# A 16-expert layer computed routed instead of dense: rows listed by expert in pieces of 64, two pieces per pass

## The reference

```python
scores = jax.nn.softmax(h @ gate_w.T, axis=-1)
topk_w, topk_idx = jax.lax.top_k(scores, 6)
cw = zeros((T, 16)).at[arange(T)[:, None], topk_idx].add(topk_w)
for e in range(16):
    g = h @ w_gate[e].T                       # 256 -> 176
    u = h @ w_up[e].T                         # 256 -> 176
    y = y + cw[:, e:e + 1] * (silu(g) * u @ w_down[e].T)
```

## Time and profile before

| | |
|---|---|
| median of 3 runs | 858.1 us (857.93 to 858.56) |
| profiled execution | 859.15 us, its span 857.4 us |
| granted clock of TensorE, mean | 0.988 |
| busy: TensorE, its weight loads | 814.1, 570.0 us |
| busy: VectorE, ScalarE, GpSimd | 457.1, 318.5, 161.8 us |
| DMA | 72.07 MB, mean 84 GB/s |

### The profile page before, as it was taken

One profiled execution on the slowest core, in us unless ns is written; L12 is line 12 of the kernel. 1 busy time (PEld: TensorE's weight loads), 2 busy tenths in 40 slices (PEclk: granted clock), 3 DMA queues, 4 the chain that ended last, 5 costly groups with the idle time before them and its releaser, 6 DMA issues.

```text
span 857.4 us, 12754 instructions
## 1 busy us (share of the span) xinstructions
PE 814.1 (95%) x4543; PEld 570.0 (66%) x4543; DVE 457.1 (53%) x1054; ACT 318.5 (37%) x651; POOL 161.8 (19%) x256
## 2 busy tenths in 40 slices
PE   6988799889969999999999999999999999999998
PEld 3566566676657786677777777777766655555557
DVE  5999866766522226866464566467443252322223
ACT  3987777545113324442423334333402211111111
POOL 3643744112510034111111111111100000000000
PEclk9998999999989999999999999999999999999999
DMA  4002780091253322022101011101123344344431
GB/s 141 2 2 34 240 269 2 22 255 33 84 169 105 93 68 68 19 62 87 31 26 37 25 38 29 33 25 37 52 94 120 119 123 124 126 154 130 134 100 49
DMA packets 63958, 72.07 MB, mean 84 GB/s; under 512 B 14201, under 2 KB 48505, under 8 KB 63897
## 3 DMA queue, kind: packets, MB, share of 16 engines
q1 hardware_dynamic: 59048, 64.06, 24.8%
q0 software_dynamic: 1536, 4.20, 1.5%
q10 hardware_dynamic: 3312, 3.02, 1.1%
HBM read 55.45 MB, written 14.75 MB: 82 GB/s over the span
## 4 chain that ended last, share of the span: by engine, by line
PE 77%; DVE 10%; issue 4%; ACT 4%; POOL 2%; DMA 2%; SPq 0%; DVEq 0%; ACTq 0%; POOLq 0%
PE bank L936 10%; PE bank L898 10%; PE bank L912 10%; PE bank L1113 8%; PE bank L1080 7%; PE bank L975 6%; PE bank L961 6%; PE bank L636 3%; PE bank L1863 3%; PE bank L658 2%; PE bank L1847 2%; PE bank L1820 2%; PE bank L1648 2%; PE bank L985 1%; DVE sh L2401 1%
## 5 line engine op out<-in xcount | busy, mean ns | idle before, releaser
L1145 ACT ACTIVATE arena<-bank 128x512 f32<-128x512 f32 (+1 forms) x64 | 34.7, 544 | 217.6 <-PE bank L898 205.5
L1253 DVE TENSOR_TENSOR arena<-arena,bank 128x512 f32<-128x512 f32 (+1 forms) x47 | 30.7, 654 | 151.7 <-PE bank L912 151.7
L936 PE MATMUL bank<-arena 128*128 128x256 f32 x448 | 108.9, 384 | 1.4 <-DVE arena L1251 1.3
L936 PEld LDWEIGHTS bank<-arena 128*128 128x128 f32 x448 | 85.8, 193 | 32.1 <-issue 20.1
L898 PE MATMUL bank<-xnT,arena 128*128 128x512 f32 (+1 forms) x256 | 107.0, 540 | 0.0
L912 PE MATMUL bank<-xnT,arena 128*128 128x512 f32 (+1 forms) x256 | 106.6, 539 | 0.0
L1214 ACT ACTIVATE arena<-bank 128x512 f32<-128x512 f32 (+1 forms) x96 | 46.8, 524 | 135.2 <-PE bank L1080 135.2
L861 POOL TENSOR_TENSOR arena<-arena,causal_t 128x256 f32<-128x256 f32 x64 | 45.1, 725 | 238.7 <-ACT arena L1219 238.7
L912 PEld LDWEIGHTS bank<-xnT,arena 128*128 128x128 f32 x256 | 48.6, 190 | 47.6 <-issue 45.9
L1113 PEld LDWEIGHTS bank<-arena 128*128 128x128 f32 x640 | 76.3, 191 | 4.4 <-POOL arena L861 2.9
L1113 PE MATMUL bank<-arena 128*128 128x129 f32 x640 | 77.0, 275 | 1.9 <-POOL arena L861 1.9
(11 more groups left out here) (236 smaller groups left out, 1178.8 us busy)
## 6 DMA issues: line engine op xcount, KB each, us to landing
arena<-in_w_gu SPq DMA_DIRECT2D x60, 256.0 KB, 3.6
rows_in<-place SPq DMA_DIRECT2D x5, 1664.0 KB, 14.6
arena<-in_w_dn SPq DMA_DIRECT2D x56, 128.0 KB, 3.5
arena<-in_wq SPq DMA_DIRECT2D x32, 128.0 KB, 2.2
arena<-in_wo SPq DMA_DIRECT2D x32, 128.0 KB, 2.0
arena<-cw_rows SPq DMA_DIRECT2D x15, 256.0 KB, 3.5
arena<-rows_in SPq DMA_DIRECT2D x23, 128.0 KB, 2.1
rows_out<-arena ACTq DMA_DIRECT2D x23, 128.0 KB, 1.7
```

The costliest lines, as they stand in the source:

```text
L936: mm = nc.tensor.matmul(Y[s][half][l // 2][:, (l % 2) * DIM:(l % 2 + 1) * DIM], hh[:, M % 3, j * P:(j + 1) * P], w_dn[:, slot_of(M), :], s ...
L1145: nc.scalar.activation(sg[:, M % 2, 0:n], ring(M)[0][:, 0:n], ACT.Silu).then_inc(s_silu, 1)
```

## The change

The layer is routed. For each half the 512 x 6 = 3,072 (token, expert) pairs are listed by expert, every expert's list rounded up to pieces of 64 rows: at most 64 pieces, so NP1 = 32 passes of two pieces, 64 passes J for both halves. In a pass, piece u (0 or 1) has the array's columns 64u to 64u + 63 and its own expert's weights.

- Routing: `route_b3` now ends in a mask; `places1` counts ranks and totals (TensorE), `rows1_read`, `rows1_index`, `rows1_weights`, `rows1_edges`, `rows1_table`, `rows1_owner` (VectorE) make the row index of each pair, its weight, and a table of weight offsets per piece. Half 0 has this in attention heads 20 to 28, its norm and logits three to four heads earlier than before; half 1 in passes 2 to 16.
- Rows: GpSimd scatters the normed rows (1,088 bytes, with a code for token and rank) into `rows1` by 24 indirect DMAs per half: four behind the masks of each of heads 25 to 30 for half 0, all 24 in pass R0 = 10 for half 1, groups of four waiting for the one before. SyncE fills `rows1` with zeros before (16 DMAs, heads 2 to 17), reads a pass's 128 rows (`load_rows`, five ahead), and reads back the codes (`ext`).
- Weights: all 16 experts' weights are loaded once, in heads 2 to 23, and stay. ScalarE and VectorE copy piece 1's (704 columns, 88 x 512) to a fixed place each pass (`pair_copy_gu`, `pair_copy_dn`), at an offset read into a register; TensorE reads two offsets per pass for piece 0.
- Results: a pass's 128 rows are copied out of PSUM (`pair_y`) and scattered by GpSimd to `ret` in token order (`send_back`); SyncE reads the six results of a half's tokens back (`load_back`, half 0 in pass 50, half 1 after the last), and VectorE adds them with their weights, 24 adds per half (`add_back`), half 0's in passes 52 to 63.
- Gone: the tile loop of the layer, the spreading of weights by DMA, `cw_turn`, `cw_evac`.

The diff, cut to its core:

```diff
+        def pair_gate_up(self, pe, J, off):
+            pe.wait_ge(s_pxe, NB + J + 1)
+            if J < 2:
+                pe.wait_ge(s_th, 3 * NH - 2 + J)
+            else:
+                pe.wait_ge(s_pm, NB + J - 1)
...
+            pe.wait_ge(s_wbg, J + 1)
+            wide = lambda w: w.rearrange("p (y k n) -> p k y n", y=2, k=KD)
+            w = wide(w1_gu[:, bass.ds(off[0], GU1)]), wide(wbg[:, J % 2, :])
+            for k in range(KD):
+                for u in range(2):
+                    mm = nc.tensor.matmul(p_gu[J % 2][u * HR:(u + 1) * HR, 0:2 * FE].rearrange("p (y n) -> p y n", y=2),
+                                          pxT[:, J % 2, k, u * HR:(u + 1) * HR], w[u][:, k, :, :],
+                                          start=(k == 0), stop=(k == KD - 1), skip_group_check=True)
+            mm.then_inc(s_pgu, 1)
...
+        def pair_down(self, pe, J, off):
+            pe.wait_ge(s_pte, NB + J + 1)
...
+            pe.wait_ge(s_wbd, J + 1)
...
+            for q in range(2):
+                for u in range(2):
+                    mm = nc.tensor.matmul(p_y[u * HR:(u + 1) * HR, :], phT[0:HB, J % 2, q, u * HR:(u + 1) * HR],
+                                          w[u][:, q, :], start=(q == 0), stop=(q == 1), skip_group_check=True)
...
+        def pair_y(self, act, J):
+            act.wait_ge(s_pyd, NB + J + 1)
+            if J >= NY:
+                act.wait_ge(s_ret, RE0 + 64 * ((J - NY) // 4 + 1))
+            nc.scalar.copy(py[J % NY], p_y).then_inc(s_pye, 1)
...
+        def send_rows(self, pool, h, groups):
+            for g in groups:
+                if g == 0:
+                    pool.wait_ge(s_pl, DI1[h])
...
+                else:
+                    pool.wait_ge(s_rows, SC + SC1 * h + 64 * g)
+                for i in range(4 * g, 4 * g + 4):
+                    nc.gpsimd.indirect_dma_start(rows1[h], bass.IndirectOffsetOnAxis(ap=sidx1[:, h, i % K1, i // K1:i // K1 + 1], axis=0),
+                                                 xa[h][:, i // K1, :], None).then_inc(s_rows, 16)
+
+        def send_back(self, pool, J):
+            h, j = J // NP1, J % NP1
+            if j == 0:
+                pool.wait_ge(s_rx1, h + 1)
+            if J and J % 4 == 0:
+                pool.wait_ge(s_ret, RE0 + 16 * J)
+            pool.wait_ge(s_pye, NB + J + 1)
...
                 if n < NH - 1:
                     self.queries(pe, n + 1)
                 else:
-                    self.gate_up(pe, F1, attn0)
+                    self.pair_turn(pe, 0)
                 if n:
                     self.project(pe, n - 1)
...
+                if n == NH - 1:
+                    self.pair_turn(pe, 1)
+                    offs = [owners(J) for J in range(3)]
+                    self.pair_gate_up(pe, 0, offs[0])
...
+            for J in range(2 * NP1):
+                if J + 2 < 2 * NP1:
+                    self.pair_turn(pe, J + 2)
+                if J + 1 < 2 * NP1:
+                    self.pair_gate_up(pe, J + 1, offs[J + 1])
+                if J + 3 < 2 * NP1:
+                    offs.append(owners(J + 3))
+                self.pair_hidden(pe, J)
+                if J:
+                    self.pair_down(pe, J - 1, offs[J - 1])
...
+            self.pair_silu(act, 0)
+            for J in range(2 * NP1):
+                if J + 2 < 2 * NP1:
+                    self.pair_copy_gu(act, J + 2)
+                    self.pair_x(act, J + 2)
+                if J + 1 < 2 * NP1:
+                    self.pair_silu(act, J + 1)
+                if J:
+                    self.pair_y(act, J - 1)
+                if J == 3:
                     self.ln_std(act, 10)
                     self.ln_std(act, 11)
...
+            for J in range(2 * NP1):
+                if J == R0:
+                    self.send_rows(pool, 1, range(K1))
+                self.send_back(pool, J)
```

More of the change, by code:

```diff
@@ L338, in cuts_of @@
         return [(a, b, min((i * P + a) // F, MOE_GATES[s] - 1)) for a, b in zip(cuts, cuts[1:])]
-    pieces = {M: cuts_of(1, IT[M][2]) for M in range(F1, F1END)}
     NBL = [16 * ((NB - j + 2) // 3) for j in range(3)]
-    cb_n = {M: NBL[M % 3] + 16 * sum(len(pieces[m]) for m in range(M, F1 - 1, -3)) for M in range(F1, F1END)}
     LEAD = 3
@@ new lines, in pick, with rows1_read @@
+        def pick(self, dve, c, src):
+            for k in range(K1):
+                ins = nc.vector.scalar_tensor_tensor(out=c.tk[:, k, :, :], in0=c.lg[:], scalar=float(k), in1=src,
+                                                     op0=ALU.is_equal, op1=ALU.mult)
+                s_r.by(ins)
+            dve.wait_ge(s_r.sem, s_r.n)
+        def rows1_read(self, dve, h):
+            dve.wait_ge(s_pf, 2 + h + 1)
+            nc.vector.tensor_copy(scr[2 + h].pos_cnt, p_pos[h][:, 0:5 * E1]).then_inc(s_pl, 1)
@@ new lines, in owner, with pair_copy_gu @@
+        def owner(self, eng, J, u, y):
+            h, q = J // NP1, 2 * (J % NP1) + u
+            if q == u:
+                eng.wait_ge(s_tab, 3 + 2 * (h + 1))
+            return eng.value_load(tab1[0:1, h, y, q:q + 1], min_val=0, max_val=(E1 - 1) * (GU1, 2 * DIM)[y])
+        def pair_copy_gu(self, act, J):
+            off = self.owner(act, J, 1, 0)
+            if J >= 2:
+                act.wait_ge(s_pgu, NB + J - 1)
+            elif J == 0:
+                act.wait_ge(s_qr, len(order))
+                act.wait_ge(s_we, n_we1)
+            nc.scalar.copy(wbg[:, J % 2, :], w1_gu[:, bass.ds(off, GU1)]).then_inc(s_wbg, 1)
@@ L749, in sp, with load_back @@
+        def load_back(self, sp, h):
+            sp.wait_ge(s_ret, RE0 + 16 * (h + 1) * NP1)
+            for k in range(K1):
+                sp.dma_start(ys[k], ret[h][1 + k * HALF:1 + (k + 1) * HALF, :].rearrange("(t p) d -> p t d", p=P)).then_inc(s_ys[k], 16)
         def sp(self, sp, attn0):
@@ L902, in up @@
         def up(self, pe, M, attn0):
[L903 removed]
+            half, i, c0, n, L = IT[M]
             cols = slice(half * HALF + c0, half * HALF + c0 + n)
[L905 to L909 removed]
+            if 2 <= M < F0B:
                 self.done(pe, M - 2)
@@ L1052, in pe @@
             pe.wait_ge(s_one, 5)
+            owners = lambda J: [self.owner(pe, J, 0, y) for y in range(2)]
             for n in range(NH):
@@ L1422, in make_rest @@
+                if NP1 + 20 <= J < 2 * NP1:
+                    for i in range(2 * (J - NP1 - 20), 2 * (J - NP1 - 19)):
+                        self.add_back(dve, 0, i)
+            for i in range(4 * K1):
+                self.add_back(dve, 1, i)
     return Rest()
```

549 lines of the change are left out of this document (360 added, 189 removed).

## The result

The changed kernel takes **867.9 us** (median of 5 runs, 865.1 to 868.7) against 858.1 (857.9 to 859.4): 1.0109 times as long, 95% interval 1.0093 to 1.0124. Slower by 1.1%, as forecast (868). The profiled execution took 867.91 us for its span of 866.1.

What follows compares the result with a forecast made beforehand. TensorE was taken to bound the kernel. Loop start 633, loop 208.5, stalls 7 and tail 19.4 gave a span of 867.9, so a median of 868 us against 858; range 850 to 884, the main forecast's own 859 to 877.

Steps and rivals of the forecast that it cites:

- One pass, 3.19: New layer's pass on TensorE: 2.49 us as the first layer's 128-row pass (the twin), plus 0.70 for four shape changes.
- rival one: Pass: the round of evacuation, copy, transposes and reads decides at 2.95 us, shape changes hide; 853 us, chance 0.22.
- The return to full width: Pass on TensorE: each change from 64-wide products back to full-width transposes loses 0.2 us.
- Do the others keep up?: Pass: ScalarE, VectorE and the queues stay below TensorE's 3.19 us; the longest round takes 2.95, leaving a cover of 0.24.
- rival two: Pass: the queues decide, register reads a third dearer give 3.4 us a pass; 881 us, chance 0.14.
- The attention heads: Heads: routing moves earlier and grows, each piece under the 4 us VectorE has free in a head; 1 us counted.
- The seam: Last head to second expert layer: TensorE stands from 617.20 to 621 for rows, then waits for six reads; loop starts at 633.
- The clock's 2 us: Seam: TensorE's stop also lowers the granted clock; 2 us added, moving the loop start from 631 to 633.
- Stalls of 7: Loop: 5 us for two changes of ScalarE's table and back, 2 us for VectorE's routing of half 1.
- Rival three: Loop: GpSimd's 24 scatters of half 1 take 41 us, pass 26's evacuation waits for returns; 876 us, chance 0.1.
- The tail: After the last product: evacuation, scatter, first read, 24 VectorE adds and output all exposed, 19.4 us.
- Rival four: Pass: the two column groups don't run side by side, 2.05 us more a pass; 999 us, chance 0.02.

Runs made afterwards that it cites:

- e1: Changed kernel with gate/up and projection at full width, the second piece's own weights left out, so no change of shape: 856.6 us (one run).
- e10: Changed kernel with e7's pass, e4's heads and e5's seam, scatters of half 1 still all before the return of pass 10: 848.4 us, 0.9895 of the kernel before.
- e2: Changed kernel with one more, unused, register read per pass in TensorE's queue, three instead of two: 869.6 us (one run).
- e4: Changed kernel with only the routing work in the attention heads reordered (norm of head 17, masks and index work of head 24): 862.1 us, 1.0050.
- e0: The changed kernel run again without an edit, as a control: 866.9 us, 1.0099 of the kernel before.
- e5: Changed kernel with head 30's projection and head 31's values before the first rows' transposes, six register reads moved into heads 29 to 31: 870.6 us, 1.0146.
- e3: Changed kernel with the transposes of input and hidden put together, two changes of shape per pass instead of four: 864.1 us, 1.0075.
- e7: e3 with a pass's two register reads apart, one behind gate/up and one behind the projection: 875.3 us, 1.0196 of the kernel before.
- e9: Changed kernel with the tail's adds shared: for the fourth tile ScalarE multiplies and GpSimd adds instead of VectorE: 879.3 us, 1.0244.
- e6: e1 with GpSimd's 24 scatters of half 1 spread in six groups over passes 13 to 23: 868.8 us (one run).
- e12: e10 with R0 13 for 10, the scatters of half 1 behind the returns of passes 10 to 12: 864.8 us, 1.0077 of the kernel before.
- e8: Changed kernel with e7's pass, e4's heads, e5's seam and e6's spread scatters together: 853.4 us, 0.9941 of the kernel before.

## Why the prediction was right, point by point

The time was right to 0.1 us, and that is luck, for two of its terms were not right. They cancelled: the loop started 5.7 us later than forecast (638.7 for 633) and took 8.1 less (207.4 for 215.5); the tail 0.6 more. The span came out at 866.1 for 867.9. Even the last step helped: 867.9 + 1.75 - 1.05 is 868.6, not 868, and the profiled execution was the median one instead of 1.05 above it. The direction hung on the same luck: with the pass as measured and the heads at the 1 us of the forecast the time would have been about 861, 0.3% above the kernel before.

- **One pass, 3.19; measured 3.07.** The mechanism holds: e1 without the changes of shape is at the twin's 2.49, e10 with half of them at 2.79. The pass lies outside the 3.15 to 3.25 that were to show it, and 0.04 above the 3.03 at which rival one would have won. The return to full width was over-priced, 0.2 from the 128-column products of the earlier trace rows where 0.15 is paid; 0.12 x 62 = 7.4 us. The Trainium skill's rule (TensorEngine Tiling (Array Packing), Key Properties: a change of tiling mode drains the engine) agrees with these traces, which give it a size.
- **Do the others keep up? They do.** ScalarE's copy took 0.78 (I had 0.85). The cover was called thin, 0.24 a pass. It is wider: e2's third read fits into it, and in e1 the pass fell 0.5 before anything else showed. So rival one (the round at 2.95) was mis-sized and rival two (the queues) falls.
- **The attention heads, "I count 1 us"; measured 8.1.** This is the step that failed. That every piece is under the 4 us that VectorE has free in a head was nearly true (the longest, the index work of head 24, took 4.2) and did not answer the question, which is what stands behind a piece in VectorE's order. The masks stood ahead of products that TensorE makes first in its head, the index work ahead of the copy of the turned head that TensorE projects, and one half's norm ahead of transposes that wait for it (1.7 us in head 18). e4 moved them, with the same work, and got 6.3 us back, some 1.7 of it clock; 1.8 us are not explained. By the same clock the 8.1 was 6.4 in e0 and 9.8 in e5.
- **The seam, 15.2 from the turned head to the loop; measured 14.75.** As forecast, with the stand of 3.26 (forecast 3.8) and the low clock. The clock's 2 us are paid where the low clock falls on gate/up and the values (in e2, e3, e7 and e9 on these two alone: the projection behind the stand took 1.89, TensorE then stood 2.9 us for the reads in its queue, and the seam was as long). In e0 it fell on the projection alone, beside which the reads go on, and the seam was 1.8 shorter. e5 and e10 show that the rest was order: 6 us of it (4 against e0's) go when work that is ready fills the stand and the six reads lie in the heads before.
- **Stalls of 7; measured 3.4** up to pass 16, at the table loads and VectorE's routing. TensorE waits 6.0 in the whole loop; the other 2.6 are 1.5 at passes 26 and 27 (next point) and 1.1 in the last passes, which the forecast had in another term.
- **Rival three came true in small.** The 24 scatters and their waits took 691.4 to 731.6, 40 us as worked out (41), and pass 26's evacuation waited 3.31 us; TensorE lost 1.7. In e1 the same hand-over took 11.6.
- **The tail, 19.4; measured 20.0 to 20.3:** 24 adds 0.44 apart for 0.43.
- **Rival four falls,** by the steady pass: eight records of 352 columns in 1.40. The rule of the Trainium skill named beside it (TensorE: Matmul & The Clock Gate, What overlaps and what doesn't) would, read strictly, hold each group's weight load back behind the other group's product; here the measurement decides.

Of the 20 us between the changed kernel's median and e10's, the profiled executions show 6.3 in the heads, 5.9 in the seam and 11.0 in the loop, 23 in all (span 866.1 against 842.0, whose own time, 843.8, is at the low end of e10's runs).

## What to carry to other kernels

Free time of an engine, summed over a stretch, is no cover: ask of each piece that is put into it which instruction now stands behind it, and who waits for that one. Where narrow products alternate with full-width ones, put those of one shape next to each other, and register reads where each has a product of its own to hide under. A cheaper pass is worth only what the slowest chain beside it allows: count what a ring of buffers waits for before the pass is shortened. Repeat the unchanged kernel before a difference of 2 us is read: here one stand cost 0, 1.7 or 3.4 us of clock by the execution.

## What was not expected of the hardware

- **Semaphores can come late.** In e5, e6, e7, e9 and e12 the projection's semaphore was updated up to 8 us after its last record ended, nearly always in passes 13 to 37, while indirect DMAs followed each other on GpSimd; TensorE's own records went on. (The end of a product's record is modelled, so the products themselves may have ended later.) Updates of the transposes' and gate/up's semaphores, and of VectorE's and ScalarE's, are late or missing in these traces too. In the changed kernel (twice), e1 to e4, e8 and e10 the hand-over took 0.05 us in all passes from 13 to 37 but 26 and 27. The five ran on two chips; e0 to e4, e8 and e10 ran on two others, and for the changed kernel's first run no chip is noted. In the loop it goes with 7 to 20 us more, and the kernel before, on the same two chips, took its usual 857.6 and 858.0.
- **It goes with the chip or the execution, not with the edits,** as far as traces can tell. The first expert layer is the same in all kernels, and GpSimd issues indirect DMAs there too (about 213 to 238 and 311 to 335 us). In the trace of the kernel before, 29 of the 195 semaphore updates by the engines in 205 to 245 and 305 to 340 us are not there within 0.3 us of their instruction's end; in the five traces 31 to 34; in the other eight none, and in no trace is one missing elsewhere before 570 us. So the kernel before, which has none of the edits, shows the same mark. No wait is longer there (TensorE stands 5.90 us for the first rows in the kernel before, 5.8 in the changed one); the time goes only in the loop. Why one chip does it and another does not stays open, and so does what the changed kernel would take on such a chip.
- **A short stand can cost clock.** After the 2.46 us in head 24, the same in nine executions, the eight score products took 3.57 to 3.98 instead of 2.32 in seven, 4.61 in one (e5, granted clock 0.72 over 12 us) and 2.41 in one (e0). After 3.26 us idle in the seam the granted clock was 0.58 over 10.6 us, so for most of it at the lower level of 1.2 GHz; in e2, after 3.34 us idle, it was still full for the next 5.3 us.
- **GpSimd's drain is long.** The last instruction of its queue took 10.0 to 10.4 us in the changed kernel, e9 and e10, and 4.2 in the kernel before. Under the work of other engines it costs nothing; in e9, where its end is bare, the program ends 4.2 us later for it.
- **GpSimd's adds slow VectorE's.** An add of 128x256 beside one of GpSimd took 0.86 to 0.99 us instead of 0.48. The Trainium skill (SBUF — State Buffer, SBUF: two separate sides) has it as an exclusive lock on a port pair that the two engines share, which a VectorE operation with two inputs in SBUF needs too, and the later one waits; the doubled adds agree.
